# Two edits between the layers of a graph transformer: rows scaled behind a block's last maxima, and three score banks for the last two blocks

## The reference

```python
def layer(x, adj, w_qkv, w_proj, b_proj, w1, b1, w2, b2, g1, be1, g2, be2):
    q, k, v = split(layer_norm(x, g1, be1) @ w_qkv)          # 8 heads of 16
    scores = einsum('nhd,mhd->hnm', q, k) * HEAD_DIM ** -0.5
    scores = where(adj != 0, scores, -inf)
    out = einsum('hnm,mhd->nhd', softmax(scores), v)
    x = x + out @ w_proj + b_proj
    return x + gelu(layer_norm(x, g2, be2) @ w1 + b1) @ w2 + b2

x = layer(layer(x, adj, ...), adj, ...)
```

## Time and profile before

| | us |
|---|---|
| median of three runs | 3415.17 (3414.4 to 3416.05) |
| the profiled execution | 3412.07 |
| its span | 3410.3 |
| mean granted clock of TensorE | 0.961 |
| PE busy | 3270.1 (96%) |
| DVE busy | 2743.7 (80%) |
| POOL busy | 2540.5 (74%) |
| ACT busy | 2431.6 (71%) |

### The profile page before, as it was taken

One profiled execution on the slowest core, in us unless ns is written; L12 is line 12 of the kernel. 1 busy time (PEld: TensorE's weight loads), 2 busy tenths in 40 slices (PEclk: granted clock), 3 DMA queues, 4 the chain that ended last, 5 costly groups with the idle time before them and its releaser, 6 DMA issues.

```text
span 3410.3 us, 71081 instructions
## 1 busy us (share of the span) xinstructions
PE 3270.1 (96%) x22132; PEld 1433.5 (42%) x22152; DVE 2743.7 (80%) x8786; ACT 2431.6 (71%) x3557; POOL 2540.5 (74%) x1536
## 2 busy tenths in 40 slices
PE   6999999999999999999788999999999999999978
PEld 3434344444434343432444444444444444444326
DVE  6888888888889898981366899999999999999514
ACT  3278797878878797978332577777777777777853
POOL 4177888787878788889321588888888888888960
PEclk7699999999999999999887899999999999999989
DMA  8687887878797978874354647565656565666422
GB/s 230 202 274 232 268 266 247 264 237 283 230 290 223 292 221 284 253 245 144 90 138 112 199 150 202 153 196 161 189 167 185 170 182 173 179 176 176 144 86 72
DMA packets 498262, 680.96 MB, mean 200 GB/s; under 512 B 60768, under 2 KB 278240, under 8 KB 497888
## 3 DMA queue, kind: packets, MB, share of 16 engines
q1 hardware_dynamic: 497600, 676.30, 65.4%
q10 hardware_dynamic: 288, 0.10, 0.0%
HBM read 512.07 MB, written 164.10 MB: 198 GB/s over the span
## 4 chain that ended last, share of the span: by engine, by line
PE 83%; issue 6%; DVE 2%; POOL 2%; DMA 2%; SPq 2%; POOLq 1%; ACT 1%; DVEq 0%; ACTq 0%
PE PS L701 28%; PE PS L684 20%; PE PS L708 17%; PE PS L714 14%; DVE spill L1130 2%; POOL arena L1356 1%; PE PS L762 1%; PE PS L622 1%; POOLq L1313 1%; ACT arena L995 1%; DMA q_t<-max_dram 1%; PE PS L827 0%; POOL arena L1319 0%; PE PS L637 0%; PE PS L817 0%
## 5 line engine op out<-in xcount | busy, mean ns | idle before, releaser
L1130 DVE CUSTOM_DVE_ANT_0 spill<-PS,mask_n 128x512 bf16<-128x512 f32 x4096 | 2595.9, 687 | 344.6 <-PE PS L684 333.0
L995 ACT ACTIVATE arena<-PS 128x512 f32<-128x512 f32 (+1 forms) x3072 | 2134.7, 740 | 614.4 <-PE PS L708 374.2
L1356 POOL TENSOR_TENSOR arena<-arena,mask 128x1024 int32<-128x1024 int32 x896 | 2132.1, 2380 | 422.8 <-ACT arena L995 359.8
L684 PE MATMUL PS<-k_t,q_t 48*128 48x512 f32 x4096 | 1658.4, 532 | 39.2 <-DVE pmax L1130 34.1
L708 PE MATMUL PS<-q_t,k_t 50*128 50x512 f32 x4096 | 1258.8, 486 | 13.6 <-DMA q_t<-max_dram 10.8
L714 PE MATMUL PS<-arena,idb 64*128 64x512 bf16 x4304 | 1150.4, 389 | 0.0
L701 PE MATMUL PS<-arena,v_sb 128*32 128x512 f32 x8192 | 1095.2, 607 | 8.6 <-POOL arena L1356 8.3
L684 PEld LDWEIGHTS PS<-k_t,q_t 48*128 48x128 f32 x4096 | 602.6, 191 | 973.2 <-DVE pmax L1130 913.4
L708 PEld LDWEIGHTS PS<-q_t,k_t 50*128 50x128 f32 x4096 | 594.9, 188 | 212.0 <-issue 114.6
L714 PEld LDWEIGHTS PS<-arena,idb 64*128 64x128 bf16 x4304 | 311.0, 94 | 376.2 <-PE PS L714 230.2
L1130 DVE DVE_READ_ACCUMULATOR2_ANT pmax<- 128x1 f32 x4096 | 342.1, 84 | 0.0
(11 more groups left out here) (54 smaller groups left out, 671.5 us busy)
## 6 DMA issues: line engine op xcount, KB each, us to landing
mask<-m_dram SPq DMA_DIRECT2D x768, 256.0 KB, 2.8
mask_n<-mn_dram SPq DMA_DIRECT2D x768, 128.0 KB, 2.9
adj_in<-in_adj SPq DMA_DIRECT2D x256, 256.0 KB, 4.4
mask<-in_adj_t SPq DMA_DIRECT2D x256, 256.0 KB, 4.2
m_dram<-mask SPq DMA_DIRECT2D x256, 256.0 KB, 3.8
mn_dram<-mask_n SPq DMA_DIRECT2D x256, 128.0 KB, 4.4
mt_dram<-arena SPq DMA_DIRECT2D x256, 128.0 KB, 3.7
arena<-mt_dram SPq DMA_DIRECT2D x256, 128.0 KB, 2.7
```

The costliest lines, as they stand in the source:

```text
L684: pe.matmul(ps_a[:, a_bank(L, n), :], q_t[r0:r0 + KROWS, gb % Q_SLOTS, pair, q * P:(q + 1) * P], k_t[r0:r0 + KROWS, pair, mb * TILE:(mb + ...
L995: nc.scalar.activation(p_buf[:, t % P_SLOTS, heads, :], ps_b[:, heads, :], ACT.Exp, scale=SCALE).then_inc(exped[part], 1)
L1130: dve.tensor_tensor_reduce(spill[:, bank, :], ps_a[:, bank, :], mask_n[:, v % N_SLOTS, :], 1.0, LOWEST, ALU.subtract, ALU.max, pmax[:, p % ...
L1356: pool.tensor_tensor(p, p, m, ALU.mult).then_inc(p_masked, 1)
```

## The change

`norm_rows` with the bias add is cut out of `add_attention` and becomes `norm_attention`. In `feed_and_project` it now stands behind `take_block(g - 3, 6, 8)`, the block's last four maxima. In rounds 0 to 2 no maxima lie between, and in `feed_forward` the two calls follow each other, so that the order stays as it was there. Scores 96 to 127 (`BESIDE` onward, blocks 6 and 7) go round all three banks. PE first waits until bank 5's last users are done: `lo_part` and `v_kept`, both counted by ACT. `a_before` looks back over six scores, since a bank's last user can lie further back where the rotation changes.

```diff
--- before.py
+++ after.py
@@ -251,13 +251,16 @@
         def hidden_bank(gi, f):
             return job_bank("h", gi, f) if gi < NB else 4 + f
 
+
+        BESIDE = (NB - 2) * NS * 4
+
         def a_bank(L, n):
 
-            return 1 + n % 2 if L > 0 and n < UNITS else (L * NSC + n) % A_BANKS
+            return 1 + n % 2 if L > 0 and n < BESIDE else (L * NSC + n) % A_BANKS
 
         def a_before(L, n):
 
-            for m in range(n - 1, max(n - 4, -1), -1):
+            for m in range(n - 1, max(n - 7, -1), -1):
                 if a_bank(L, m) == a_bank(L, n):
                     return L * NSC + m + 1
             return 0
@@ -901,7 +904,9 @@
                     score_block(M, g - 3, 7)
                     if g >= 1:
                         project_v(gp, ORDER["p", M, g - 1])
-                for n in range((NB - 2) * NS * 4, NB * NS * 4):
+                pe.wait_ge(lo_part, 4 * NB)
+                pe.wait_ge(v_kept, 2 * NB)
+                for n in range(BESIDE, NB * NS * 4):
                     score_a(M, n)
 
             pe.wait_ge(wp_here, 16)
@@ -1236,6 +1241,8 @@
                 dve.tensor_tensor(x2, PS[:, 2, :], x2, ALU.add).then_inc(proj_taken, 1)
                 dve.drain()
                 norm_stats(x2v, gx)
+
+            def norm_attention(gi, gx):
                 norm_rows(x2v, gx)
                 dve.tensor_tensor(x2_b[:, gi % 2, :].rearrange("p (t c) -> p t c", t=NS), x2v, row_bias(C_B2), ALU.add)
                 dve.drain()
@@ -1254,12 +1261,14 @@
                 for g in range(2):
                     normalise(gi0 + g)
                     add_attention(gi0 + g, ORDER["f", L, g])
+                    norm_attention(gi0 + g, ORDER["f", L, g])
                 for g in range(NB):
                     if g + 2 < NB:
                         normalise(gi0 + g + 2)
                     add_ff(gi0 + g)
                     if g + 2 < NB:
                         add_attention(gi0 + g + 2, ORDER["f", L, g + 2])
+                        norm_attention(gi0 + g + 2, ORDER["f", L, g + 2])
 
             def feed_and_project(L):
                 gi0, M = L * NB, L + 1
@@ -1284,6 +1294,8 @@
                     if g + 2 < NB:
                         add_attention(gi0 + g + 2, ORDER["f", L, g + 2])
                     take_block(g - 3, 6, 8)
+                    if g + 2 < NB:
+                        norm_attention(gi0 + g + 2, ORDER["f", L, g + 2])
                 for n in range((NB - 2) * NS * 4, NB * NS * 4):
                     take_max(M, n)
```

## The result

The changed kernel takes 3399.31 us in the median of seven runs (3395.04 to 3404.7), beside 3414.4 us for the kernel before (3408.09 to 3416.05). The ratio is 0.9957, with a 95% interval of 0.9946 to 0.9967: about 14.7 us faster. The direction was forecast, but 22.5 us were expected, and the time lies 0.3 us above the range. The profiled execution takes 3399.31 us, its span is 3397.5 us.

A forecast was written before the change was run, and what follows sets the result against it. The prediction took PE, waiting for maxima behind DVE's scaling and POOL between the layers, as the bound. Gains of 17.9 + 4.6 = 22.5 us from 3415.17 gave 3392.7, stated as 3393 us, range 3388 to 3399.

The forecast's parts named there:

- the wait that is left: PE's stall before the last score pair of rounds 3 to 5, forecast to fall from 5.98 to 1.95 us.
- the moved rows at no cost: Scaling behind the last maxima in rounds 3 to 5: costed at nothing, at most 0.2 us a round without cover.
- the tail: The stage's last 32 maxima: with three banks 19.6 us instead of 24.99, less 0.8 us added wait, gain 4.6 us.
- provided that the clock stays up through 1.95 us of idleness: Condition on the clock gain in rounds 3 to 6: PE's remaining stall would leave the granted clock at 1.00.
- part one: Scaling the rows behind the maxima in rounds 3 to 5: 15.6 us plus 2.25 us of clock, 17.9 us.
- 2.25 us named as such: Clock gain at the fronts of rounds 4, 5 and 6: 1.18, 0.67 and 0.4 us at full clock.
- 5.2 us a round: Ends of rounds 3 to 5: line 628 to next hidden layer takes 4.82 us instead of 10.00, three times, 15.6 us.
- one row, one wait without a fall: Profile row 1714 to 1717: PE idle 1.92 us, clock 1.00 there and in the 3 us behind it.
- The first rival: Clock falls in rounds 3 to 5 despite short stalls; only stalls and tail gain, 16.7 us, 3398.5; chance 0.12.
- the row on 1834 to 1843: Profile row cited for short gaps lowering the clock: 0.63 with PE busy 7.10 of 9.00 us, no long stall.
- The other rivals: Tail keeps its pace (3395 to 3398, 0.15); rows only move the wait (3410.6, 0.03); second attention's clock rises later (3423, 0.02).
- part two: Third bank for the tail's 32 maxima: 5.4 us less, 0.8 us added wait, gain 4.6 us.

The follow-up runs named there:

- filled: Changed kernel plus two matmuls of no use in each PE wait of rounds 3 to 5; 3395.1, 3389.1, 3388.4 us in three runs.
- bank_only: Changed kernel with norm_attention put back ahead of the maxima, leaving only the three banks and their waits; 3414.1 us, 0.9998 of the kernel before.
- rows_only: Changed kernel without the three banks and their waits, leaving only the moved row scaling; 3403.9 us, 0.9970 of the kernel before.
- deferred: Changed kernel with the row scaling moved into the next round, behind normalise; 3401.1 us, 0.9966 of the kernel before.
- behind_all: As deferred, with add_attention and its statistics also moved behind the last four maxima; 3392.3 us, 0.9942 of the kernel before.
- slotted_near: Changed kernel with the scaling between pieces 3 and 4 of the next round's maxima, add_attention left ahead of the last four; 3387.8 us, 0.9923.
- half_filled: As filled, but one matmul of no use in each place instead of two; 3394.7 us, 0.9941 of the kernel before.
- slotted: As behind_all, but with the scaling between pieces 3 and 4 of the maxima, where DVE stands idle; 3379.9 us, 0.9899 of the kernel before.

## Why the prediction was wrong

- **Read rightly:** the bound (PE waiting for maxima behind DVE's scaling and POOL), the wait that is left (1.95 us forecast; 2.02, 2.04 and 2.34 measured), the moved rows at no cost, and the tail (4.6 us, measured 4.6). The 2.34 us belong to round 5, where the kernel before has the same 0.38 us more in DVE's statistics; the prediction took all three rounds as alike.
- **The step that failed** is "provided that the clock stays up through 1.95 us of idleness". Of the 17.9 us of part one, 12.1 are the shorter waits and 5.8 the clock: 2.25 us named as such, and the full-clock paces of `project_v` and the scores inside "5.2 us a round". The shorter waits came, at 11.5 us; that the comparison at full clock gives 12.1 as in the sum is luck, since 0.6 of it lies in rounds 7 and 8. On balance nothing of the 5.8 came: the half clock costs 7.1 us now where it cost 6.0. The 1.1 us more are about what one fall costs (1.15 us in filled's second trace), and the wait of 2.3 us early in round 3, which was there before, is now followed by one.
- **Why it failed:** the step rested on one row, one wait without a fall. Over the traces with such waits between 1.79 and 2.36 us in rounds 3 to 6 (before, bank_only, the changed kernel twice, rows_only, deferred, behind_all, slotted_near), 22 of 26 are followed by a fall. They are not 26 independent cases, since some kernels share their code or repeat. The row of before was one of the four exceptions, and bank_only at the same place is another.
- **The first rival was the case:** 16.7 us, 3398.5 forecast, 15.6 us in the trace and 3399.3 measured. Its mechanism, a short wait that still costs the clock, is what filled and half_filled show. The Trainium skill's "TensorE: Matmul & The Clock Gate", section "A second HAM failure mode: psum-queue depth-cycling", which spoke for it with short idle times as banks are cycled, agrees with these traces in that the clock falls without a long gap, behind waits of 1.17 to 1.51 us; here they come once or twice a round and not between all groups. The rival had a chance of 0.12, and the row on 1834 to 1843, 0.63 with no long stall, should have weighed more: its longest wait is 0.90 us.
- The other rivals did not happen: the keys were in time, nothing held the maxima, and the second attention stage took the same time.
- Open: when a given short wait is followed by a fall and when not. The wait of 2.3 us early in round 3 was followed by a fall in both traces of the changed kernel and in rows_only, and by none in before and bank_only, with the same code up to there in all five; slotted and behind_all differ behind waits of 1.04 us. No run here tells what decides it.

## What to carry to other kernels

Shortening PE's waits to 2 us was worth their length here and no more. The clock came back where a wait vanished or was filled up to 0.8 us or less, and hardly ever where 1 us or more was left. So price the two separately, and take the clock's part only for a wait that all but vanishes. Where it can't vanish, filling it with matmuls of no use shows within one run what the clock is worth. An operation that is on nobody's path belongs where its own engine is idle. With the same scaling PE waited 6 us a round at one place and 4 us (deferred) at another. In an idle stretch of DVE, and with the statistics behind the last maxima as well, it hardly waited at all (slotted).

## What the runs showed that was not expected

- Waits of PE of 1.17 to 1.51 us were each followed by 3 us or more at clock 0.50 (half_filled). Of the 26 falls behind the waits of 1.17 to 2.36 us counted above, 17 start 1.0 to 2.3 us after PE is at work again, the other nine within 0.7 us. The instructions that pay are then often not those next to the wait.
- Some 5.3 us of fillers in each of three waits cost nothing, since they ran in idle time, and made the kernel before faster by 0.0016 of its time (0.9984, 0.9974 to 0.9995).
- The medians of one kernel on three chips differ by several us (filled 3388.4 to 3395.1), more than part two is worth. The length of the rounds in the trace repeated to 0.01 us in the changed kernel and to 0.02 us between before and bank_only; filled differed by 0.4 us without a fall in rounds 3 to 6, and by 1.15 us with one.
